# Split fp32r query projections in two narrow attentions, and normalised rows of the int8 feed-forward made in the attention before it

## The reference, cut to what matters

```python
x = x + attention_L0(layernorm(x), ctx, ...)      # 16 heads of 16
x = x + fp8_product(layernorm(x))
x = x + attention_L1(layernorm(x), ctx, ...)      # 16 heads of 64
x = x + top2_experts(layernorm(x))
x = x + transformer_block(layernorm(x), ctx)
x = x + expert_choice(layernorm(x))
x = x + attention_L3(layernorm(x), ctx, ...)      # 16 heads of 16
x = x + int8_ffn(layernorm(x))

def attention_L3(q, k, v, mask, Wq, bq, ...):
    qw = q @ Wq + bq                              # 2048 x 256 by 256 x 256
    scores = heads(qw) @ heads(k @ Wk + bk).T * scale + mask * NEG
    return softmax(scores) @ heads(v @ Wv + bv) @ Wo + bo

def act_fake_quant(x, clip):
    scale = sigmoid(clip) * max(abs(x)) / 127     # max over ALL tokens
    return clip_(round(x / scale), -128, 127) * scale

def int8_ffn(x):
    xq = act_fake_quant(x, clip_x)
    h = act_fake_quant(silu(xq @ q(w_gate).T) * (xq @ q(w_up).T), clip_down)
    return h @ q(w_down).T
```

## Time and profile before

| | us |
|---|---|
| three runs | 1690.39, 1685.46, 1683.31 |
| profiled execution | 1688.04 |
| its span | 1686.2 |
| start-up of L0, until its loop over tiles (PE) | 0 to 44.25 |
| start-up of L3, from its first DVE work until its loop (PE) | 1455.5 to 1491.94 |
| loop of L3 | 1491.94 to 1591.5 |
| int8 stage, until the first product of its first layer | 1592.6 to 1611.3 |
| its first layer, then second scale and second layer | 1611.3 to 1651.6, to the end |

### The profile page before, as it was taken

How to read it: one execution, slowest core, us unless ns; L and a number is a source line. 1 busy time by engine, 2 the same in 40 slices (tenths; PEclk the granted TensorE clock), 3 DMA queues, 4 the chain that set the end, 5 groups by cost and what they waited for, 6 DMA issues and landing times. The chain is left out here.

```text
span 1686.2 us, 25577 instructions
## 1 busy us (share of the span) xinstructions
PE 1427.7 (85%) x9564; PEld 1205.4 (71%) x9573; DVE 1103.0 (65%) x2349; ACT 759.5 (45%) x1305; POOL 642.7 (38%) x439
## 2 busy tenths in 40 slices
PE   6997769997759999996899997669999999499774
PEld 4786558897559999995677776247888888368632
DVE  6676767987556677773465554776667665467487
ACT  2454555553137676762445333113343343155465
POOL 1452135566124555542132223023655564244100
PEclk9899889999979999997899998879999999799797
DMA  5000000000356777755000000433444442500001
GB/s 189 1 1 6 1 1 1 1 1 1 126 190 195 217 226 218 222 142 124 21 1 1 1 1 0 140 101 82 97 98 91 109 75 42 116 1 2 1 1 50
DMA packets 94177, 122.04 MB, mean 72 GB/s; under 512 B 12300, under 2 KB 79271, under 8 KB 94055
## 3 DMA queue, kind: packets, MB, share of 16 engines
q1 hardware_dynamic: 72935, 91.56, 16.9%
q0 software_dynamic: 21120, 28.85, 9.5%
HBM read 94.95 MB, written 25.43 MB: 71 GB/s over the span
## 5 line engine op out<-in xcount | busy, mean ns | idle before, releaser
L2672 POOL DMA_INDIRECT ch_total<-ch_y,ch_index x64 | 107.1, 1673 | 122.8 <-DVE ch_y L2859 107.9
L1276 POOL DMA_INDIRECT t_total<-t_y,t_index x46 | 99.4, 2161 | 132.5 <-DVE t_y L1395 122.5
L3674 POOL TENSOR_TENSOR L_s<-L_s,L_mx 128x1232 f32<-128x1232 f32 x32 | 76.5, 2391 | 128.9 <-DVE L_mx L3758 128.9
L2796 ACT ACTIVATE ch_silu<-ch_ps 128x512 f32<-128x512 f32 x64 | 38.4, 599 | 170.0 <-PE ch_ps L800 160.5
L798 PE MATMUL ch_ps<-ch_hT_hi,ch_w_hi 128*128 128x512 f32 x256 | 103.5, 404 | 11.0 <-DVE ch_hid L2885 7.6
L798 PE MATMUL t_ps<-t_hT_hi,t_w_hi 128*128 128x256 f32 x368 | 106.8, 290 | 6.1 <-DVE t_w_lo L1383 6.1
L798 PE MATMUL t_ps<-t_w_hi,t_act_hi 128*128 128x256 f32 x368 | 105.8, 288 | 0.0
L799 PE MATMUL t_ps<-t_hT_lo,t_w_hi 128*128 128x256 f32 x368 | 105.7, 287 | 0.0
L800 PE MATMUL t_ps<-t_hT_hi,t_w_lo 128*128 128x256 f32 x368 | 105.7, 287 | 0.0
L800 PE MATMUL t_ps<-t_w_hi,t_act_lo 128*128 128x256 f32 x368 | 104.1, 283 | 0.0
L799 PE MATMUL t_ps<-t_w_lo,t_act_hi 128*128 128x256 f32 x368 | 104.1, 283 | 0.0
(11 more groups left out here) (589 smaller groups left out, 4513.4 us busy)
## 6 DMA issues: line engine op xcount, KB each, us to landing
t_w_in<-in_L_ffn_w1T SPq DMA_DIRECT2D x23, 1024.0 KB, 5.0
t_w_in<-in_L_ffn_w2T SPq DMA_DIRECT2D x23, 1024.0 KB, 5.7
ch_w_in<-in_L_ffn_w SPq DMA_DIRECT2D x24, 512.0 KB, 3.8
x<-in_x SPq DMA_DIRECT2D x4, 512.0 KB, 4.9
t_total<-x SPq DMA_DIRECT2D x1, 2048.0 KB
t_rows<-t2d_h SPq DMA_DIRECT2D x1, 2048.0 KB
...
```

The source lines that it names most:

```text
L1276: nc.gpsimd.indirect_dma_start(out=total, out_offset=bass.IndirectOffsetOnAxis(ap=index[:, 2 * j + u:2 * j + u + 1], axis=0), in_=y[:, j % ...
L2672: nc.gpsimd.indirect_dma_start(out=total, out_offset=at(s, u), in_=y[:, s % 2, u, :], in_offset=None, compute_op=ALU.add).then_inc(added[s ...
L3674: nc.gpsimd.tensor_tensor(s[:, n % G], s[:, n % G], spread(mx[:, n % G, :], 2, [P, H, KEYS]), ALU.subtract).then_inc(shifted, 1)
```

## The change

There are two parts. In both narrow attentions the query projection becomes a `split_matmul`. ACT now writes `hT_hi` where it wrote `hT`, and additionally `wq_hi`; DVE gets `wq_lo` once and `hT_lo` for each group (`rows_rest`). The second part moves work of the int8 stage. `NormalRows` owns the normalised rows; the moments of tiles 0 to 11 are computed by DVE in step 13 of the loop of L3, their rows by ACT in steps 13, 14 and 15 (four tiles each), their maxima by DVE one step later. The int8 stage then handles only tiles 12 to 15. The maximum over the partitions goes over a PE transpose in place of POOL's instruction. The down weights are turned inside the first layer, after its second chunk, and the fillers are 10 instead of 34.

```diff
+class NormalRows:
+    GROUPS = NG - 1
+    def moments(self, chain, st, tiles):
+        row_moments(nc, chain, tiles, st, self.mv, self.var, self.rstd, self.tmp)
+        nc.vector.scalar_tensor_tensor(out=self.shift[:, ts], ...).then_inc(self.moments_ready, 1)
+    def normalise(self, act, x, t):
+        act.wait_ge(self.moments_ready, t // (self.GROUPS * G) + 1)
+        self.nc.scalar.activation(self.h[:, t, :], x[:, t, :], ACT.Identity, ...).then_inc(self.rows_ready, 1)
+    def peak(self, g):
+        self.nc.vector.tensor_reduce(self.peaks[:, g:g + 1], rows, AX.X, ALU.max, ...).then_inc(self.peaks_ready, 1)
@@ int8_feed_forward: PE
-            for c in range(IC):
-                turn(WD_TURN + c)
...
-            keep_busy(nc, ps[:, 3, 0:2 * P], k.ident[:].bitcast(BF16), 34)
+            pe.wait_ge(top_ready, 1)
+            nc.tensor.transpose(ps[:, 2, 0:P], top_wide[:], k.ident[:]).then_inc(top_turned, 1)
+            keep_busy(nc, ps[:, 3, 0:2 * P], k.ident[:].bitcast(BF16), 10)
...
+                    if g == 0 and c == 1:
+                        for m in range(IC):
+                            turn(WD_TURN + m)
@@ int8_feed_forward: ACT
-            for j in range(W1_TURNS):
-                take(j)
-            act.wait_ge(moments_ready, 1)
-            for t in range(HALF_T, NT):
-                nc.scalar.activation(h[:, t, :], k.x[:, t, :], ACT.Identity, ...)
-            for c in range(IC):
-                take(WD_TURN + c)
+            take(0)
+            take(1)
+            for t in (NT - 2, NT - 1):
+                normal.normalise(act, k.x, t)
@@ int8_feed_forward: DVE
-            row_moments(nc, chain, range(NT), k.st, mv, var, rstd, tmp)
-            nc.vector.tensor_reduce(top[:, 0:1], h[:].rearrange("p t d -> p (t d)"), AX.X, ALU.max, ...)
+            normal.moments(chain, k.st, range(LAST_T, NT))
...
+            normal.peak(NG - 1)
+            dve.wait_ge(normal.peaks_ready, NG)
+            chain(nc.vector.tensor_reduce(top[:, 0:1], normal.peaks[:], AX.X, ALU.max))
+            nc.vector.tensor_copy(top_wide[:], top[:, 0:1].broadcast_to([P, P])).then_inc(top_ready, 1)
+            dve.wait_ge(top_turned, 1)
+            chain(nc.vector.tensor_reduce(amax_all[:, 0:1], ps[:, 2, 0:P], AX.X, ALU.max))
@@ narrow_attention: PE
             def queries(g):
-                pe.wait_ge(hT_ready, g + 1)
-                pe.wait_ge(q_loaded, 32)
+                pe.wait_ge(hT_lo_ready, g + 1)
+                pe.wait_ge(wq_lo_ready, 1)
...
-                        ins = nc.tensor.matmul(ps[:, 6 + c, :], wq[:, kc, c * P:(c + 1) * P], hT[:, g % 2, kc, :], ...)
+                        ins = split_matmul(nc, ps[:, 6 + c, :], (wq_hi[...], wq_lo[...]), (hT_hi[...], hT_lo[...]), ...)
@@ narrow_attention: ACT
-                nc.scalar.copy(hT[:, g % 2], ps[:, 4:6, :]).then_inc(hT_ready, 1)
+                nc.scalar.copy(hT_hi[:, g % 2], ps[:, 4:6, :]).then_inc(hT_hi_ready, 1)
             act.wait_ge(q_loaded, 32)
+            nc.scalar.copy(wq_hi[:], wq[:]).then_inc(wq_hi_ready, 1)
@@ narrow_attention: DVE
+            def rows_rest(g):
+                dve.wait_ge(hT_hi_ready, g + 1)
+                if g >= 2:
+                    dve.wait_ge(q_psum, (g - 1) * HC16)
+                nc.vector.tensor_tensor(hT_lo[:, g % 2], ps[:, 4:6, :], hT_hi[:, g % 2].bitcast(F32), ALU.subtract)
...
+            dve.wait_ge(wq_hi_ready, 1)
+            nc.vector.tensor_tensor(wq_lo[:], wq[:], wq_hi[:].bitcast(F32), ALU.subtract).then_inc(wq_lo_ready, 1)
...
             take(0)
             normalise(range(NT - G, NT))
+            rows_rest(2)
             take(1)
+            rows_rest(3)
             take(2)
             for n in range(NT):
...
+                if normal and n == NT - NormalRows.GROUPS:
+                    dve.wait_ge(next_ready, NormalRows.GROUPS * G)
+                    normal.moments(chain, k.st, range(0, NormalRows.GROUPS * G))
+                if normal and n > NT - NormalRows.GROUPS:
+                    dve.wait_ge(normal.rows_ready, (g + 1) * G)
+                    normal.peak(g)
```

More of the change, by code:

```diff
@@ L3024, in round, with __init__, allocate, sb @@
                                  ).then_inc(self.w_rounded, 1)
+class NormalRows:
+    GROUPS = NG - 1
+    def __init__(self, nc):
+        self.nc = nc
+    def allocate(self, ctx):
+        def sb(name, shape, dt=F32):
+            return ctx.enter_context(self.nc.sbuf_tensor("qr_" + name, shape, dt))
+        self.h, self.mv, self.peaks = sb("h", [P, NT, D]), sb("mv", [P, NT, 2]), sb("peaks", [P, NG])
+        self.var, self.rstd, self.tmp, self.shift = (sb(n, [P, NT]) for n in ("var", "rstd", "tmp", "shift"))
+        sem = Semaphores(self.nc, ctx, "qr_")
+        self.moments_ready, self.rows_ready, self.peaks_ready = sem("moments"), sem("rows"), sem("peaks")
+    def moments(self, chain, st, tiles):
+        nc, ts = self.nc, slice(tiles[0], tiles[-1] + 1)
+        row_moments(nc, chain, tiles, st, self.mv, self.var, self.rstd, self.tmp)
+        nc.vector.scalar_tensor_tensor(out=self.shift[:, ts], in0=self.mv[:, ts, 0], scalar=-1.0, in1=self.rstd[:, ts],
+                                       op0=ALU.mult, op1=ALU.mult).then_inc(self.moments_ready, 1)
+    def normalise(self, act, x, t):
+        act.wait_ge(self.moments_ready, t // (self.GROUPS * G) + 1)
+        self.nc.scalar.activation(self.h[:, t, :], x[:, t, :], ACT.Identity, bias=self.shift[:, t:t + 1],
+                                  scale=self.rstd[:, t:t + 1]).then_inc(self.rows_ready, 1)
+    def peak(self, g):
+        rows = self.h[:, g * G:(g + 1) * G, :].rearrange("p t d -> p (t d)")
+        self.nc.vector.tensor_reduce(self.peaks[:, g:g + 1], rows, AX.X, ALU.max, apply_absolute_value=True
+                                     ).then_inc(self.peaks_ready, 1)
 def clip_rounded(nc, chain, v, out):
@@ L3032, in clip_rounded, with int8_feed_forward @@
     chain(nc.vector.tensor_scalar(out, v, ROUNDER, None, ALU.subtract))
-def int8_feed_forward(nc, k, i, out, down):
+def int8_feed_forward(nc, k, i, out, down, normal):
     with ExitStack() as ctx:
@@ L3087, in int8_feed_forward @@
                                                        for kc in range(KC)], D))
-        for g in range(NG):
+        for g in range(1, NG):
             rows_turned(g)
@@ L3222, in _ @@
                         round_rows(g + 2)
+                    if g == 0 and c == 1:
+                        for m in range(IC):
+                            take(WD_TURN + m)
                     if c == 3 and g + 1 < NG:
@@ L3371, in narrow_attention @@
         var, rstd, tmp = sb("var", [P, NT]), sb("rstd", [P, NT]), sb("tmp", [P, NT])
-        h, hT = sb("h", [P, NT, D]), sb("hT", [P, 2, KC, GT])
+        h = sb("h", [P, NT, D])
+        hT_hi, hT_lo = sb("hT_hi", [P, 2, KC, GT], F32R), sb("hT_lo", [P, 2, KC, GT], F32R)
+        wq_hi, wq_lo = sb("wq_hi", [P, KC, D], F32R), sb("wq_lo", [P, KC, D], F32R)
         qT = sb("qT", [P, HC16, T])
@@ L3507, in queries @@
                     for kc in range(KC):
-                        ins = nc.tensor.matmul(ps[:, 6 + c, :], wq[:, kc, c * P:(c + 1) * P], hT[:, g % 2, kc, :],
-                                               start=(kc == 0), stop=(kc == KC - 1))
+                        ins = split_matmul(nc, ps[:, 6 + c, :],
+                                           (wq_hi[:, kc, c * P:(c + 1) * P], wq_lo[:, kc, c * P:(c + 1) * P]),
+                                           (hT_hi[:, g % 2, kc, :], hT_lo[:, g % 2, kc, :]),
+                                           start=(kc == 0), stop=(kc == KC - 1))
                     ins.then_inc(q_psum, 1)
@@ L3656, in _ @@
                     exponential(n + 2)
+                if normal and n >= NT - NormalRows.GROUPS:
+                    g = n - (NT - NormalRows.GROUPS)
+                    for t in range(g * G, (g + 1) * G):
+                        normal.normalise(act, k.x, t)
             output_turned(NT - 1)
@@ L3725, in _ @@
                                             ).then_inc(kbd_ready, 1)
+            rows_rest(0)
             statistics(range(NT // 2, NT))
@@ L3736, in _ @@
             values_taken(1)
+            rows_rest(1)
             dve.wait_ge(o_loaded, 48)
```

59 lines of the change are left out of this document (34 added, 25 removed).

## The result

| | before | after |
|---|---|---|
| median of 9 runs each | 1684.45 us | 1692.47 us |
| lowest to highest | 1681.64 to 1690.39 | 1685.65 to 1702.68 |
| ratio after to before | | 1.0047, 95% interval 1.0029 to 1.0065 |
| profiled execution | 1688.04 us | 1692.41 us |
| its span | 1686.2 us | 1690.6 us |

The changed kernel is about half a per cent slower. The forecast was 1688.3 us, 2.8 us above before; the median lies 8.0 us above. That is inside the range, but outside the 0 to 5 us that had the chance of 0.50.

What follows compares the result with a forecast made beforehand. No engine fills the span; DVE bounds the start-ups, ACT's rows and DVE's maximum the int8 start. Terms 6.8 + 0.1 - 5.5 + 1.0 + 0.4 = +2.8 on 1685.5 gave 1688.3 us, range 1681 to 1694.5.

Steps and rivals of the forecast that it cites:

- The passes: Query projections on PE: twelve fp32r passes per group take 2.80 us, saving 0.64 us per group at full clock.
- The rests on the start-ups: Both narrow attentions' start-ups: added DVE operations make the loops start 3.1 and 3.7 us late, +6.8 us together.
- The end of the loop: Last attention's final steps: moved moments, rows and maxima fit into idle time, +0.1 us, from 0 to +4.
- The rival bound of +4: Last attention's end: upper bound of that term, each such step costing up to 2 us if the cover were gone.
- The int8 start: Int8 stage: rounding 6.95 us earlier, 0.7 and 0.8 given back in the first layer, -5.5 us, bounds -7.2 and -3.
- The clock term: Start-ups: new PE gaps lower the clock ahead of groups 0 and 2, +1.0 us, from -3 to +5.
- my terms without the clock: Whole kernel: start-ups +6.8, loop end +0.1, int8 start -5.5, semaphores to clear at the end +0.4; 1.8 us.
- the forecast's signs of being wrong: Passes over 0.24 us apart, longer L3 loop, DVE idle mid-start-up, or first layer slower than 1.38 us per chunk after group 0.
- Rests hide: Start-ups: DVE's idle time covers the rests and PE saves 0.64 us per group; result below before, chance 0.28.
- Int8 part gives nothing: Int8 stage: ACT or PE, not the maximum, sets the first layer's start; 1694 us, chance 0.05.
- Lower clock in the start-ups: Groups 0 and 2 of the queries: 2.3 us for each group at 1.2 GHz; 1695 us, chance 0.17.

Runs made afterwards that it cites:

- the kernel without rests: Split queries in both attentions with high parts read in place of both rests, int8 stage as before, against the kernel before: ratio 1.0011, +1.5 us.
- the int8 part alone: fp32 queries as before, rows and maxima of the int8 stage as in the change, against the kernel before: ratio 0.9970, -4.7 us.
- the second comparison: The whole change unedited, run once more beside other runs of the kernel before: ratio 1.0027, +4.4 us in the mean.
- the split alone: Three fp32r query passes with rests in both narrow attentions, int8 stage as before, against the kernel before: ratio 1.0062, +12.2 us.
- rests without passes: Casts and rests of the split kept, PE multiplying in fp32, int8 stage as before, against the kernel before: ratio 1.0088, +16.7 us.
- the doubled rests: Split queries, int8 stage as before, each hT_lo computed twice on DVE, against the kernel before: ratio 1.0135, +22.8 us.

## Why the prediction was right in its range, and what it missed

- **The passes.** Forecast 0.64 us per group, at starts 0.23 apart. The rows after show 0.23 (1476.92, 1477.15), the kernel without rests 0.62 per group. The Trainium skill's rule of four passes for a true fp32 product (page "FP8 and Floating Point Precision", section "TensorE Precision Notes") would have made it some 0.9 us, an estimate; the trace, 0.86 us per product, decides here too.
- **The rests on the start-ups.** Forecast for the last attention: second statistics 2.35 us late, group 2 3.1 us late, loop 39.5 us after the first statistics. Measured 2.6, 3.03 and 40.61. First attention: 3.7 forecast for the statistics, 3.35 measured (3.53 from the first statistics); loop 48, measured 48.84. The steps hold, and doubling or removing the rests moves the start-ups the way they say. Shown. The size is short: against the profile of before the start-ups are 4.8 and 4.2 us longer, 9.0 in sum, where 6.8 and 1.0 for the clock were forecast.
- **The clock in the start-ups** is where they end later than forecast. Group 3 in the last attention took 4.13 us (1501.12 to 1505.25) and not 2.8. Group 2 in the first took 4.44. In the first attention the comparison of profiles hides a part of it: 37.75 us before held a fall of its own, at a PEclk of 0.91 in the window of before below, against 0.95 in the int8 part alone. The four other start-ups with fp32 queries and no fillers took 36.11 to 36.29, so the split's 42.5 is 6.3 us more, where the steps at full clock give 3.7. In the last attention three such start-ups took 35.31 to 35.36, so 40.61 is 5.3 us more and not 4.2. The forecast took the profile of before as its base, in which group 1 of the queries took 5.83 us (3.70 at full clock) and, in the first attention, 6.26; in the int8 part alone it was 5.40 and 4.61.

```profile
6.50:44.25 37.75, 31.02 (x148) 18.93 (x149) 29.74 (x92) 10.94 (x15) 8.68 (x17) 0.91 0.51 174
```

- **The end of the loop.** Forecast +0.1; the rows after show that nothing was pushed. The rival bound of +4 didn't come.
- **The int8 start.** Forecast -5.5. Rounding 6.9 us sooner, as predicted (6.95); from the stage's start to the second scale 5 us are left in the profile, and the part alone gained 4.7 us in the runs. What is given back lies in the layer's first group, as forecast: from its first product with the SiLU on DVE to that of the second group it takes 11.40 us for 9.73, 1.7 us more, where 0.7 and 0.8 were forecast; behind it DVE goes at 1.38 us per chunk as before. One thing the forecast's sum holds without saying it: the small maximum, the transpose and its maximum took 1.31 us until the scale (1609.11 to 1610.42), as forecast, but POOL's instruction in the old kernel needed 0.54 (from the maximum's end at 1605.72 to 1606.26), so that sub-step gave away 0.8 us. Of before, the rows for it:

```profile
1605.85 0.38 POOL L3120 PARTITION_ALL_REDUCE q_amax_all<-q_top  x1 [12.09 <-DVE q_top L3269]
1606.26 0.16 DVE L3255 SCALAR_TENSOR_TENSOR q_x_scale<-q_amax_all,q_clip 128x1 f32<-128x1 f32 x1 [0.55 <-POOL q_amax_all L3120]
```
- **The clock term is the one that was mis-sized.** It stood at +1.0 with bounds -3 and +5, for the start-ups only. The kernels with a split ran at a mean clock lower by 0.0014 to 0.0056 in the whole run. That is not theirs alone: the int8 part with fp32 queries is at -0.0017, and each of these differences is uncertain by 0.0015 to 0.0028 (95%). For the whole change it is 0.0022, at 1.4 us per 0.001 some 3.0 us. Taken off the 4.4 us of the second comparison, 1.4 us are left, where my terms without the clock gave 1.8. That they agree so well is partly luck: with the clock taken off in the same way, the split alone costs 10.3 us, where my terms gave 6.8 and 0.4, and the int8 part gives 7.1, where they gave 5.4. Both terms were too small, and in the sum their errors cancel in part; the parts then make 3.2 us and the whole 1.4, a difference that the intervals cover. In the first comparison the clock of before was not recorded beside the times; its 8.0 us are more than the second's and may in part be the luck of the draw. Whether the lower clock is a fixed consequence of the work or of where the falls lie is open: rests without passes and passes without rests both have it.
- **The signs.** One of the forecast's signs of being wrong came in the profile after: DVE idle in the middle of both start-ups, 0.76 and 1.69 us ahead of `wq_lo`. In the first attention the forecast had this wait for ACT's cast in its step (`wq_lo` from 15.93, as measured), so the step stands.
- **The rivals.** "Rests hide" is refuted by the rows and by the doubled rests. "Int8 part gives nothing" is refuted by the part alone. "Lower clock in the start-ups" had the right mechanism and not the right place: it named groups 0 and 2, and in the profile after groups 1 and 3 of the last attention and 1 and 2 of the first ran at 1.2 GHz for four to seven of their twelve passes (group 1 of both had slow products before the change too); in the second profile of the same kernel it was 0 and 2 of the last and 1 to 3 of the first. The first comparison (+8.0 us) lies nearer to this rival's 1695, the second (+4.4) nearer to the forecast. It deserved more than 0.17, and a price that reached beyond the start-ups.
